# Storing row maxima element by element instead of transposing them first, in an attention and feed-forward kernel

## What is computed

```
q = (x @ Wq.T + bq).reshape(B, S, H, Dh)        # keys are the queries
buckets = ...                                    # 6-bit hash of each (row, head)
scores = jnp.einsum('bhsd,bhtd->bhst', q, q) / jnp.sqrt(jnp.float32(E))
same = (b_hs[:, :, :, None] == b_hs[:, :, None, :]).astype(scores.dtype)
coeff = NB - 2 + same                            # 62 or 63
attn = jax.nn.softmax(scores * coeff, axis=-1)
out = jnp.einsum('bhst,bhtd->bhsd', attn, v)
```

## Time and profile before

| | us |
|---|---|
| median of three executions | 1377.42 |
| the three executions | 1378.29, 1373.04, 1377.42 |
| span of the profiled execution, first to last instruction | 1378.0 |
| PE busy | 1223.5 (89%) |
| DVE busy | 1225.7 (89%) |
| ACT busy | 1084.6 (79%) |
| POOL busy | 1221.7 (89%) |

### The profile page before, as it was taken

How to read it: one execution, slowest core, us unless ns; L and a number is a source line. 1 busy time by engine, 2 the same in 40 slices (tenths; PEclk the granted TensorE clock), 3 DMA queues, 4 the chain that set the end, 5 groups by cost and what they waited for, 6 DMA issues and landing times. The chain is left out here.

```text
span 1378.0 us, 19641 instructions
## 1 busy us (share of the span) xinstructions
PE 1223.5 (89%) x5302; PEld 500.2 (36%) x5394; DVE 1225.7 (89%) x3837; ACT 1084.6 (79%) x1573; POOL 1221.7 (89%) x259
## 2 busy tenths in 40 slices
PE   3666799999989999998989999998999999898897
PEld 1211234343333434333343434433343433333343
DVE  4988999999999999999999999999999999999420
ACT  2344778979797988979798897979798897979852
POOL 2699999999999999999999999999999998999810
PEclk9877999999999999999999999999999999999998
DMA  3563445444544455455544544454454535453100
GB/s 104 154 182 112 132 111 154 127 130 120 147 120 118 132 134 141 109 140 125 131 133 124 142 123 132 133 139 129 114 136 128 145 98 146 120 135 102 40 8 8
DMA packets 89470, 167.37 MB, mean 121 GB/s; under 512 B 18192, under 2 KB 54160, under 8 KB 89360
## 3 DMA queue, kind: packets, MB, share of 16 engines
q1 hardware_dynamic: 89252, 165.82, 44.6%
q10 hardware_dynamic: 108, 0.30, 0.1%
HBM read 150.59 MB, written 15.47 MB: 121 GB/s over the span
## 5 line engine op out<-in xcount | busy, mean ns | idle before, releaser
L980 POOL TENSOR_TENSOR logits<-max_row,logits 128x4096 f32<-128x4096 f32 x128 | 1138.7, 8915 | 65.6 <-DMA max_row<-max_scratch 41.0
L808 DVE CUSTOM_DVE_ANT_0 logits<-s_bank,coeff 128x512 f32<-128x512 f32 x1024 | 692.5, 676 | 0.0
L1032 ACT ACTIVATE logits<-logits 128x1024 f32<-128x1024 f32 x512 | 509.0, 1048 | 44.8 <-POOL logits L980 43.6
L758 DVE TENSOR_SCALAR coeff<-brow,bcol 128x516 bf16<-128x516 bf16 x1024 | 485.2, 474 | 36.8 <-PE s_bank L550 31.2
L550 PE MATMUL s_bank<-mov_stack,stat_stack 128*128 128x512 bf16 x932 | 324.8, 393 | 42.4 <-DVE rowmax L808 31.7
L570 PE MATMUL aux_bank<-logits,v_pad 128*32 128x512 f32 x2048 | 255.3, 618 | 39.8 <-ACT logits L1032 38.9
L701 PE MATMUL f_bank<-hid_b,h_sb 128*128 128x512 f32 x512 | 249.0, 594 | 0.9
L690 PE MATMUL f_bank<-hid_a,h_sb 128*128 128x512 f32 x512 | 246.1, 592 | 0.1
L550 PEld LDWEIGHTS s_bank<-mov_stack,stat_stack 128*128 128x128 bf16 x1024 | 93.2, 99 | 317.7 <-DVE rowmax L808 177.8
L690 PEld LDWEIGHTS f_bank<-hid_a,h_sb 128*128 128x128 f32 x512 | 96.0, 190 | 80.6 <-issue 69.3
L701 PEld LDWEIGHTS f_bank<-hid_b,h_sb 128*128 128x128 f32 x512 | 95.0, 190 | 80.8 <-issue 70.9
(11 more groups left out here) (101 smaller groups left out, 911.5 us busy)
## 6 DMA issues: line engine op xcount, KB each, us to landing
max_row<-max_scratch SPq DMA_DIRECT2D x128, 512.0 KB, 4.2
brow<-bucket_scratch SPq DMA_DIRECT2D x63, 522.0 KB, 6.3
mov_stack<-q_scratch SPq DMA_DIRECT2D x192, 96.0 KB
stat_stack<-q_scratch SPq DMA_DIRECT2D x189, 96.0 KB
max_scratch<-rowmax_T SPq DMA_DIRECT2D x512, 1.0 KB
q_scratch<-q_parts SPq DMA_DIRECT2D x16, 384.0 KB, 4.6
x_in<-in_x SPq DMA_DIRECT2D x16, 256.0 KB, 3.1
q_scratch<-q_parts SPq DMA_DIRECT2D x16, 256.0 KB, 5.1
```

Source lines behind the costliest of these rows:

```text
L758: nc.vector.tensor_scalar(coeff[:, k % 3, :].rearrange("p (r n) -> p r n", r=ROW_RUNS), brow[:, h // 4 % 2, h % 4, :, 0:RUN], bcol[:, b % ...
L808: nc.vector.tensor_tensor_reduce(out=logits[:, ring(b, k), :], in0=tile_bank(k)[:], in1=coeff[:, k % 3, 0:SEQ], scale=float(E) ** -0.5, sc ...
L980: nc.gpsimd.tensor_tensor(tiles, max_row[:, m % 2].unsqueeze(2).broadcast_to([P, GROUP, ST, SEQ]), tiles, ALU.subtract).then_inc(below_max ...
L1032: nc.scalar.activation(logits[:, first:first + 2, :], logits[:, first:first + 2, :], ACT.Exp, scale=-1.0).then_inc(probs_done, 1)
```

## The change

The transposition is taken out of DVE's program, with its two semaphores and its buffer `rowmax_T`. SP waits for `logits_done` of the group's last tile instead, and issues one DMA that takes the 128x8 maxima straight from their columns: 4 bytes from each of 8 columns in 128 partitions, to the places where the four stores put them. DVE's guard on `rowmax` now is that the store of two groups back has landed.

```diff
-        rowmax = sb("rowmax", [P, 2, P // ST])
-        rowmax_T = sb("rowmax_T", [P, 2, P // ST])
+        rowmax = sb("rowmax", [P, 2, GT])
...
-        MAXIMA_DMAS = P // 32
...
             def store_maxima(b, m):
 
-                sp.wait_ge(rowmax_T_done, b * GROUPS + m + 1)
-                for n in range(MAXIMA_DMAS):
-                    sp.dma_start(max_scratch[b, m * GROUP:(m + 1) * GROUP].rearrange("h (t s) -> (h t) s", t=ST)[:, 32 * n:32 * (n + 1)],
-                                 rowmax_T[32 * n:32 * n + GT, m % 2, :]).then_inc(maxima_stored, 16)
+                sp.wait_ge(logits_done, b * TILES + (m + 1) * GT)
+                sp.dma_start(max_scratch[b, m * GROUP:(m + 1) * GROUP].rearrange("h (t s) -> s (h t)", t=ST),
+                             rowmax[:, m % 2, :], allow_slow_non_contiguous=True).then_inc(maxima_stored, 16)
 
             def load_maxima(b, m):
 
-                sp.wait_ge(maxima_stored, 16 * MAXIMA_DMAS * (b * GROUPS + m + 1))
+                sp.wait_ge(maxima_stored, 16 * (b * GROUPS + m + 1))
...
-            nc.vector.memset(rowmax[:], 0.0).then_inc(rowmax_clear, 1)
...
-            def transpose_maxima(b, m):
-
-                dve.wait_ge(logits_done, b * TILES + (m + 1) * GT)
-                if b * GROUPS + m >= 2:
-
-                    dve.wait_ge(maxima_stored, 16 * MAXIMA_DMAS * (b * GROUPS + m - 1))
-                nc.vector.transpose(rowmax_T[:, m % 2, :], rowmax[:, m % 2, :]).then_inc(rowmax_T_done, 1)
...
                 if k % GT == 0 and n >= 2 * GT:
 
-                    dve.wait_ge(rowmax_T_done, n // GT - 1)
+                    dve.wait_ge(maxima_stored, 16 * (n // GT - 1))
...
-                if k % GT == 0 and n:
-                    transpose_maxima(*divmod(n // GT - 1, GROUPS))
```

More of the change, by code:

```diff
@@ L284, in sandwich_kernel @@
         logits_done = sem("logits_done")
-        rowmax_clear = sem("rowmax_clear")
-        rowmax_T_done = sem("rowmax_T_done")
         maxima_stored = sem("maxima_stored")
@@ L787, in attend_tile @@
                 dve.wait_ge(coeff_done, n + 1)
-                if n == 0:
-                    dve.wait_ge(rowmax_clear, 1)
                 if k % ST == 0 and n >= RING:
@@ L935, in iteration @@
                         attend_tile(i, k)
-                    if feed and not attend and k == 0:
-                        transpose_maxima(i - 1, GROUPS - 1)
                     for step in (0, 1):
```

## The result

The changed kernel takes **1950.2 us** (median of four, 1944.8 to 1953.9) against 1377.6 (1373.0 to 1378.3): 1.415 times as long, with a 95% interval of 1.412 to 1.418. The forecast was 1367, the range 1356 to 1386. Even the rival on the slow side, at 1400, stood for a loss of 22 us; the loss is 573.

What follows compares the result with a forecast made beforehand. DVE was taken to set the pace: 128 transpositions at 0.09 us gave -11.5 us, nine tenths let through made -10.3; from the profiled 1378.0, with the median 0.6 below the span, that gave 1367 us, range 1356 to 1386.

Steps and rivals of the forecast that it cites:

- The landing of the store: Between a group's last tile and its load: the new store lands 2.4 us after its issue begins, from 1.16 + 63c.
- c: In the new store: time of one 4-byte packet on a DMA engine, taken as 20 ns, ends 10 to 110.
- The price of a late load: At POOL's load of the maxima: free up to 1.5 us late, then about 15 us in all per microsecond.
- this cover at 1.5 us: At POOL's load of the maxima: a delay up to 1.5 us costs nothing.
- rival 3: At the new store: a penalty per 4-byte write or slow packet generation makes the kernel slower, 1400 us; chance 0.16.
- DVE sets the pace: In the middle of the program: time taken from DVE shortens the batch; 128 transpositions give 11.5 us, nine tenths let through.
- The reading of the overlap: In DVE's tile with a transposition: one costs 0.09 us by distance between neighbours, not the row's 201 ns duration.
- 1.00 us for the tile at the border: On DVE, sign of being right: the tile that lost its transposition takes 1.00 us like the others.
- the unchanged end: After 1289 us: the 89 us belonging to PE and ACT stay; only DVE's finish changes.
- SP's waits as the first sign of a slow store: On SP, listed among the signs of being wrong: waiting over 4 us for each store.
- DVE's new guard: On DVE's maxima buffer: never waits at 2.4 us of landing; past 9.8 us it would stop DVE.

Runs made afterwards that it cites:

- spread_store: Changed kernel with the 1024 elements stored 64 bytes apart, maxima load taken from the input, exponential scale -0.001: 1376.0 us, ratio 0.996 to the kernel before.
- write_patterns: Probe without the kernel's work, single stores to DRAM each waited for: 8.8 us for one column of 128 elements, 2.8 for 1024 elements 64 bytes apart.
- late_one: Kernel before with one more small store, waited for, between the landing of the four stores and the load of the maxima: ratio 1.031.
- late_two: Kernel before with two more small stores, each waited for, between the landing of the four stores and the load of the maxima: ratio 1.066.
- load_unwaited: Changed kernel whose broadcast load reads the input and does not wait for the slow store, exponential scale -0.001: 1684.1 us, ratio 1.219 to the kernel before.
- twice: Kernel before with each transposition done twice on DVE, first into a spare buffer: ratio 1.001.
- off_chain: Kernel before, stores taking untransposed rows once the last tile ends, transposition kept on DVE but unawaited, exponential scale -0.001: 1363.7 us, ratio 0.988.
- guard_of_four: Changed kernel with four parts of the maxima buffer instead of two, DVE's guard asking for the store of four groups back: 2054.4 us, one execution.

## Why the prediction was wrong

- **The landing of the store** is the step that failed: "it should land after about 1.16 + 63c", with c bracketed by the times of packets, 10 to 110 ns. c itself lies below the low end (7 ns), and the landing was 9.0 us alone on the queue and a wait of 10.9 on average instead of 2.4, outside even the far end of 8.1. The sum had no term for what comes behind the packets. A packet's time in the trace is not the time until its data counts as landed. The read-modify-write below 512 bytes, which the Trainium skill, "DMA: Bandwidth & Descriptors", section "Specifications", names and the prediction set against the 10 ns of the earlier trace rows, is a rule on the size of a write; spread_store shows that 131072 writes of 4 bytes do not slow the kernel as such, and write_patterns that dense ones land late. The old stores could not have shown it: each of their writes was 128 contiguous bytes. Why dense ones land late stays open.
- **The price of a late load**, "this cover at 1.5 us" and 15 us for each microsecond beyond, failed too: there is no cover and the price is 25 us (late_one, late_two). For a delay of 12.1 us (15.4 from last tile to load, against 3.3) the line gives 300 us and the kernel lost 570. Two more things act at that length, the unlanded store that also holds the loads behind it (load_unwaited) and SP's chain of one store after another; how the rest divides between them is not shown. The sum for rival 3 is also slightly off: a load 2.2 us later than before belongs to a c of about 61 ns, not 57.
- **"DVE sets the pace"** was wrong. DVE's and POOL's idle shares, 3.7% and 4.1%, could not tell the two apart; the runs do. A transposition more costs DVE 2 us in all (twice), not 11.5, and taking it off the maxima's way gains 17 (off_chain). The reading of the overlap, 0.09 us and not 0.20, was not what decided.
- **A term put at nothing**: POOL's subtraction takes 0.10 us longer in the changed kernel, some 13 us in all. The prediction has no term for it. With the store landing after 2.8 us, as in spread_store, the change comes to 1376 and not 1367, outside the forecast's own 1360 to 1370.
- **Right by their rows**: 1.00 us for the tile at the border, the unchanged end, SP's waits as the first sign of a slow store, and rival 3 as the side on which it would fail. Its mechanism, a penalty on each 4-byte write, was wrong, and its chance of 0.16 too low. DVE's new guard did stop DVE, as the text said it would past 9.8 us, but wasn't the cause (guard_of_four, in one execution).

## What to carry to other kernels

Before a store with a strided last dimension replaces a transposition, look at where its elements land: 4-byte elements side by side in DRAM landed 7 us after their packets were over, the same elements 16 bytes or more apart did not. Price a DMA by the time until its semaphore, from a row of the same pattern or from a probe, not by the packets. And where several engines are busy for about the same share, find the one that sets the pace by delaying one hand-over by a known amount and reading the slope: two runs here gave 25 us for each microsecond, which no busy share had shown.

## What the runs showed of the hardware

Dense single elements written to DRAM: 8.6 us for 128 of them, 2.3 us for 16, 1.5 us for 128 at 64 bytes; the packets' own time, 7 ns each in the first store of the changed kernel, says nothing of it. Loads issued behind such a store land behind it (`x_res`, issued 0.5 to 3.3 us behind one, after 12.1 us in the changed kernel, 2.9 before). Loads that are still under way when the store is issued come late as well: `brow`, which in the changed kernel nearly always has the next store 0.4 to 1.8 us behind it and no unlanded one ahead, landed after 9.4 us in the median instead of 6.3.

A DVE addition with two operands in SBUF that begins during a subtraction of POOL does not end before it: 7.92 us instead of 0.69. The Trainium skill, "SBUF — State Buffer", section "Who interferes with whom", says that a DVE instruction with two SBUF inputs contends with a GpSimd instruction that reads SBUF, through a port that only one of them can hold; by its section "Summary: rules for kernel authors" the one that issues second is blocked until the first has finished. By that rule the trace agrees: the addition ends 0.55 us after the subtraction. Moving work from a busy GpSimd to VectorE can cost most of a GpSimd instruction each time, here 7.6 us in the median of 16.
